# Splitting the attention's score maxima before the turn instead of after it, with two row transfers in place of six

## The reference, cut to what matters

```python
scores = jnp.einsum('bsqhd,bthd->bqhst', qh, kh) * scale
probs = jax.nn.softmax(scores, axis=-1)
a_dot = jnp.einsum('bqhst,bthd->bsqhd', probs, vh)
```

## Time and profile before

| what | value |
|---|---|
| median of 3 runs | 823.25 us (820.08 to 824.85) |
| the profiled execution, its own time | 819.99 us |
| its span in the profile | 818.1 us |
| PE busy | 734.5 us (90%) |
| DVE busy | 484.8 us (59%) |
| ACT busy | 413.3 us (51%) |
| POOL busy | 150.4 us (18%) |
| attention, first score matmul to last | 146.9 to 512.8 us |

### The profile page before, as it was taken

One profiled execution on the slowest core, in us unless ns is written; L12 is line 12 of the kernel. 1 busy time (PEld: TensorE's weight loads), 2 busy tenths in 40 slices (PEclk: granted clock), 3 DMA queues, 4 the chain that ended last, 5 costly groups with the idle time before them and its releaser, 6 DMA issues.

```text
span 818.1 us, 13465 instructions
## 1 busy us (share of the span) xinstructions
PE 734.5 (90%) x3824; PEld 345.9 (42%) x3825; DVE 484.8 (59%) x675; ACT 413.3 (51%) x803; POOL 150.4 (18%) x265
## 2 busy tenths in 40 slices
PE   4999999688888888888888888899999999998997
PEld 2455445211221222222221112466656565657887
DVE  4375688678889888888898880221212121215854
ACT  2473401477788777787787787422222222225432
POOL 1000001755532222121222121000000000003740
PEclk9999999889999999999999999999999999999999
DMA  9637100447210111110110361051111111111431
GB/s 315 215 97 289 30 0 15 137 141 236 83 57 16 30 30 30 30 29 17 29 30 30 91 207 64 27 193 47 43 51 39 51 38 51 38 39 59 120 100 51
DMA packets 51279, 65.35 MB, mean 80 GB/s; under 512 B 9497, under 2 KB 44209, under 8 KB 51249
## 3 DMA queue, kind: packets, MB, share of 16 engines
q1 hardware_dynamic: 40192, 40.85, 15.8%
q10 hardware_dynamic: 7984, 15.73, 5.8%
q0 software_dynamic: 3072, 8.39, 3.2%
HBM read 40.15 MB, written 24.38 MB: 79 GB/s over the span
## 4 chain that ended last, share of the span: by engine, by line
PE 69%; issue 9%; ACT 7%; DVE 5%; POOL 4%; SPq 3%; DMA 2%; ACTq 1%; DVEq 0%; POOLq 0%
PE ps L1291 16%; PE ps L1273 9%; PE ps L1360 8%; PE ps L1154 7%; ACT att L689 6%; PE ps L1314 6%; PE ps L1392 5%; DVE smax L938 4%; PE ps L1146 3%; PE ps L1407 3%; PE ps L1351 2%; SPq L388 2%; PE ps L1179 2%; PE ps L1114 2%; PE ps L1262 1%
## 5 line engine op out<-in xcount | busy, mean ns | idle before, releaser
L938 DVE TENSOR_REDUCE smax<-ps 128x2 f32<-128x1024 f32 x256 | 302.4, 1221 | 54.7 <-PE ps L1179 52.3
L689 ACT ACTIVATE att<-ps 128x512 f32<-128x512 f32 x512 | 267.7, 602 | 92.1 <-PE ps L1314 90.5
L1314 PE MATMUL ps<-att 51*128 51x512 bf16 x512 | 162.3, 388 | 55.2 <-ACT att L689 23.5
L1179 PE MATMUL ps<-att 48*128 48x512 bf16 x512 | 159.9, 389 | 1.4 <-DVE smax L938 1.4
L1314 PEld LDWEIGHTS ps<-att 51*128 51x128 bf16 x512 | 40.0, 94 | 244.9 <-ACT att L689 103.0
L1291 PE MATMUL ps<-big,xn 128*128 x312 | 140.9, 594 | 1.8 <-ACT oT_sb L662 1.2
L1273 PE MATMUL ps<-att,v_head 128*32 128x512 f32 x1024 | 138.8, 614 | 1.4 <-ACT o_sb L657 0.4
L1018 DVE COPY xn<-ps 128x512 f32<-128x512 f32 x39 | 27.0, 692 | 170.2 <-PE ps L1351 170.2
L1291 PEld LDWEIGHTS ps<-big,xn 128*128 128x128 f32 x312 | 58.9, 190 | 61.5 <-issue 59.7
L564 POOL DMA_INDIRECT xn<-slot_y,slot x32 | 33.7, 1054 | 237.3 <-DMA slot_y<-xn 227.9
L1360 PE MATMUL ps<-big,xn 128*128 x312 | 73.7, 380 | 0.1
(11 more groups left out here) (149 smaller groups left out, 642.8 us busy)
## 6 DMA issues: line engine op xcount, KB each, us to landing
big<-w ACTq DMA_DIRECT2D x8, 1024.0 KB, 5.8
q_stacks<-big SPq DMA_DIRECT2D x12, 512.0 KB
att<-q_stacks SPq DMA_DIRECT2D x64, 96.0 KB, 2.2
slot_x<-zeros SPq DMA_DIRECT2D x1, 4992.0 KB, 17.1
e_x<-slot_x SPq DMA_DIRECT2D x39, 128.0 KB, 2.0
slot_y<-xn SPq DMA_DIRECT2D x39, 128.0 KB, 1.7
big<-w ACTq DMA_DIRECT2D x8, 512.0 KB, 8.1
att<-k_stacks SPq DMA_DIRECT2D x64, 48.0 KB, 2.0
```

The source lines that it names most:

```text
L689: act.activation(probs[:, t % 2, g, :], ps[:, RING[turn_of(u) % 3], :], ACT.Exp, scale=SCALE)\
L938: dve.reduce_max(smax[:, s % 2, :].rearrange("p (half v) -> p half v", half=2)[:, :, v], ps[:, bank:bank + 2, :], X_AXIS).then_inc(max_don ...
L1179: return pe.matmul(ps[:, bank + half, :], q_st[s][rows, g, P * st:P * (st + 1)], k_st[s][rows, :], start=True, stop=True)
L1314: pe.matmul(ps[:, RING[turn % 3], :], k_st[s][rows, P * t:P * (t + 1)], q_st[s][rows, g, :], start=True, stop=True).then_inc(scores_ready, 1)
```

## The change

The maxima are split before they are turned. POOL's `split_max` reads `smax` (128 x 16) as soon as the eight reductions are done and writes three bf16 parts as columns of `max_parts` (128 x 48), again with four dependent instructions, now of 128 x 16 each. It stands ahead of `stage_v` in POOL's queue. PE turns all 48 columns with one bf16 matmul against a bf16 identity `eye`; it now waits for `m_ready` (POOL), not for `max_done` (DVE). ACT negates 48 x 128 into bf16 `neg_parts` and now waits for `m_loaded` of two steps before. SP waits for ACT's `negm_ready` and issues two DMAs of three rows each. POOL makes `eye` once at the start. DVE's first reduction of a step waits for `m_ready` instead of `maxT_in_psum`.

```diff
             def m_rows(i, s):
-                sp.wait_ge(m_ready, i + 1)
+                sp.wait_ge(negm_ready, i + 1)
                 for half in range(2):
-                    for c in range(3):
-                        row = HALF * half + R + c
-                        sp.dma_start(q_st[s % 4][row:row + 1, :, :].rearrange("o g s -> o (g s)"),
-                                     m_parts[8 * half:8 * half + 8, s % 2, c, :]).then_inc(m_loaded[s % 2], 16)
+                    first = HALF * half + R
+                    sp.dma_start(q_st[s % 4][first:first + 3, :, :].rearrange("c g n -> c (g n)"),
+                                 neg_parts[24 * half:24 * half + 24, s % 2, :]).then_inc(m_loaded[s % 2], 16)
...
+            pool.wait_ge(ident_ready, 1)
+            pool.tensor_copy(eye[:, :], ident[:, :]).then_inc(eye_ready, 1)
...
-            def split_m(i, s, pairs):
+            def split_max(i, s):
 
                 a = s % 2
-                pool.wait_ge(negm_ready, i + 1)
-                wait(pool, m_loaded[a], pairs * 96)
-                pool.tensor_tensor(m_parts[:, a, 0, :], negm[:, a, :], zeros[0:16, 0:P], ALU.subtract).then_inc(m_hi, 1)
+                whole, rest = [m.rearrange("p (half v) -> p half v", half=2) for m in (smax[:, a, :], max_rest[:, :])]
+                hi, mid, lo = [max_parts[:, a, :].rearrange("p (half c v) -> p half c v", half=2, c=3)[:, :, c, :]
+                               for c in range(3)]
+                nothing = zeros[:, 0:16].rearrange("p (half v) -> p half v", half=2)
+                pool.wait_ge(max_done, i * 8 + 8)
+                wait(pool, maxT_in_psum, i - 1)
+                pool.tensor_tensor(hi, whole, nothing, ALU.subtract).then_inc(m_hi, 1)
                 pool.wait_ge(m_hi, i + 1)
-                pool.tensor_tensor(negr[:, a, :], negm[:, a, :], m_parts[:, a, 0, :], ALU.subtract).then_inc(m_res, 1)
+                pool.tensor_tensor(rest, whole, hi, ALU.subtract).then_inc(m_res, 1)
                 pool.wait_ge(m_res, i + 1)
-                pool.tensor_tensor(m_parts[:, a, 1, :], negr[:, a, :], zeros[0:16, 0:P], ALU.subtract).then_inc(m_mid, 1)
+                pool.tensor_tensor(mid, rest, nothing, ALU.subtract).then_inc(m_mid, 1)
                 pool.wait_ge(m_mid, i + 1)
-                pool.tensor_tensor(m_parts[:, a, 2, :], negr[:, a, :], m_parts[:, a, 1, :], ALU.subtract)\
-                    .then_inc(m_ready, 1)
+                pool.tensor_tensor(lo, rest, mid, ALU.subtract).then_inc(m_ready, 1)
...
+            split_max(0, 0)
             stage_v(0, 0, 0, 0)
-            split_m(0, 0, 0)
...
                     if not (first and s == 0):
+                        split_max(i, s)
                         stage_v(i, b, h0 + s, s)
-                        split_m(i, s, blk * 2 + s // 2)
...
-            def negate_max(i, s):
+            def negate_max(i, s, pairs):
                 act.wait_ge(maxT_in_psum, i + 1)
-                wait(act, m_ready, i - 1)
-                act.activation(negm[:, s % 2, :], ps[0:16, RING[MAX_AT % 3], 0:P], ACT.Copy, scale=-1.0)\
+                wait(act, m_loaded[s % 2], pairs * 32)
+                act.activation(neg_parts[:, s % 2, :], ps[0:48, RING[MAX_AT % 3], 0:P], ACT.Copy, scale=-1.0)\
                    .then_inc(negm_ready, 1)
...
                 if v == 0:
-                    wait(dve, maxT_in_psum, i - 1)
+                    wait(dve, m_ready, i - 1)
...
             def transpose_max(i, s):
-                pe.wait_ge(max_done, i * 8 + 8)
+                pe.wait_ge(m_ready, i + 1)
                 bank_free(i - 1, MAX_AT)
-                pe.transpose(ps[0:16, RING[MAX_AT % 3], 0:P], smax[:, s % 2, :], ident[:, :])\
+                pe.matmul(ps[0:48, RING[MAX_AT % 3], 0:P], max_parts[:, s % 2, :], eye[:, :], start=True, stop=True)\
                   .then_inc(maxT_in_psum, 1)
...
-                pe.wait_ge(m_loaded[s % 2], blk * 192 + 96 * (s // 2 + 1))
+                pe.wait_ge(m_loaded[s % 2], blk * 64 + 32 * (s // 2 + 1))
```

More of the change, by code:

```diff
@@ L127, in build @@
         smax = sb("smax", [P, 2, 16])
-        negm = sb("negm", [16, 2, P])
-        negr = sb("negr", [16, 2, P])
-        m_parts = sb("m_parts", [16, 2, 3, P], BF16)
+        max_parts = sb("max_parts", [P, 2, 48], BF16)
+        max_rest = sb("max_rest", [P, 16])
+        neg_parts = sb("neg_parts", [48, 2, P], BF16)
+        eye = sb("eye", [P, P], BF16)
         rden = sb("rden", [P, 2, 32])
@@ L197, in build @@
         ident_ready = sem("ident_ready")
+        eye_ready = sem("eye_ready")
         consts_ready = sem("consts_ready")
@@ L676, in exps @@
                     if u == 4 and not last:
-                        negate_max(i + 1, s + 1)
+                        negate_max(i + 1, s + 1, blk * 2 + (s + 1) // 2)
                     if u == 7 and last:
@@ L697, in _ @@
             LATE = {-4: (4, 5), -3: (6,), -2: (7,), -1: ()}
-            negate_max(0, 0)
+            negate_max(0, 0, 0)
             for i in range(4):
@@ L1089, in _ @@
             pe.wait_ge(ident_ready, 1)
+            pe.wait_ge(eye_ready, 1)
             def transpose_xn(g):
```

## The result

The changed kernel took 824.59 us (median; 821.97 to 827.34). The kernel before, run beside it on the same chips, took 817.45 us (811.80 to 827.62). The ratio is 1.0083 (95% interval 1.0064 to 1.0102): slower by 0.8%, where 817.4 us and a gain had been forecast. The profiled execution took 826.23 us, its span is 824.4; against the one before, 819.99, that is 6.2 us more.

What follows compares the result with a forecast made beforehand. PE owned most of the chain of waits, with SP's issues of maxima rows 2%. Won 8.6 us, lost 2.8, net 5.8: 819.99 to 814.2 us profiled, 817.4 on the median's scale; range 809 to 825.

Steps and rivals of the forecast that it cites:

- The even stalls: PE's waits for the maxima rows at even step starts, costing about 0.54 us each; all were to go.
- S: Serial path from last reduction to turn: hand-over to POOL, four instructions, three gaps, hand-over to PE; 1.30 us.
- the wait only moves: Rival, chance 0.10: at 0.23 us per POOL instruction a pair costs 0.62, eating the 8.6 won: 823 us.
- the part on steps 1 to 5: Early steps: 2.0 us won in step 1 and 2.4 in steps 2 to 5, part stalls, part half clock ending.
- The prediction's own sign of being wrong: A pair shorter than 22.0 or longer than 23 us, step 1 starting after 160, or PE waiting for rows again.
- start of step 1: Step 1 begins at 157.6, not 161.85, as its rows land before the expert weights start: 4.2 us won.
- step 1: Step 1 falls from 12.65 us to 10.62, an odd step without the stall at its end: 2.0 won.
- steps 2 to 5: They took 46.91 us where two ordinary pairs take 44.52: 2.4 won, from stalls and half clock.
- pairs of steps, from step 6 to 27: Each pair costs 0.20 us more: odd steps 0.56 later, even ones 0.36 earlier; +2.2 us here.
- steps 28 to 30: End of the attention: the same 0.20 us lost per pair of steps, +0.2 us here.
- The early stretch gives less: Rival, chance 0.20: half clock may come from expert weights, or rows still land late behind them; about 820 us.
- Slower: Rival, chance 0.10: short POOL instructions mostly fixed cost, every turn waits for the split; 831 us at 0.30 us each.

Runs made afterwards that it cites:

- the best version: The late turn's kernel with the split for step 1 moved ahead of POOL's eight additions: 800.52 us, ratio 0.9789; on a third chip 797.16 us, ratio 0.9754.
- the kernel with filler in odd steps: Changed kernel with two unread matmuls of 384 columns before PE's wait for the split, in odd steps only: 817.10 us, ratio 1.0004.
- the fifth instruction: Changed kernel with a fifth dependent POOL instruction in the split (the second one made twice): 840.90 us, ratio 1.0278.
- six transfers: Changed kernel with six transfers of one row each again, in place of two of three rows: 824.90 us, ratio 1.0008.
- the control of the filler: Changed kernel with two unread matmuls of 384 columns before PE's wait for the split, in even steps only: 827.47 us, ratio 1.0126.
- the late turn: Changed kernel with the turn of the maxima put behind the first weighted values in PE's queue: 800.92 us, ratio 0.9717; repeated, 801.10 us, ratio 0.9793.

## Why the prediction was wrong

**What held.** The even stalls went. S was 1.24 to 1.42 us, mostly 1.32, forecast 1.30 (step 28 aside, where other waits hold the turn). The weighted values follow the turn after 0.16 us, forecast 0.155. A pair at full clock takes 22.46 to 22.54 us, forecast 22.46. Two issues take 1.47 us, forecast 1.3 to 4. POOL's instruction was mis-sized a little, 0.22 us for 0.18, which alone would have made S 1.46; the hand-over to POOL took 0.08 where 0.20 was taken, and that to PE 0.13. The nearest of the prediction's rivals in size, "the wait only moves", set the point from which a pair costs 0.62 at 0.23 us an instruction and S = 1.51; the instruction came near it and S did not. From the figures of the Trainium skill (GPSIMD Engine Reference, section 3.1) the prediction had worked out an estimate of 0.095 us. The trace does not agree with it: 0.22 us at 16 elements.

**What failed.** The step is in the part on steps 1 to 5: "I take it that it stays at 2.4 GHz when the stalls are gone, as it did in the steps that lost only 0.5 us." It was costed for those five steps and not looked at for the others. The stalls of 0.5 us were not gone but moved: an even step had lost 0.47 to 0.55 us at its start, and an odd step now loses 0.57 or 0.65 us right behind another wait of 0.89 us. Nine times out of fourteen (the odd steps 3 to 29) 3.4 us at half clock followed, 1.17 us each; with 0.50 us of the pause filled none did. The row of that wait was in the earlier trace rows. The comparison with steps "that lost only 0.5 us" took a stall by itself; here two come within 2.8 us. The prediction's own sign of being wrong came true by it: a pair of steps 6 to 27 took 23.25 us on average, above 23. The sum in the profile:

| term | forecast | measured |
|---|---|---|
| start of step 1 | -4.2 | -2.9 |
| step 1 | -2.0 | -2.4 |
| steps 2 to 5 (2.4 won, 0.4 lost to two pairs) | -2.0 | -0.9 |
| pairs of steps, from step 6 to 27 | +2.2 | +10.9 |
| steps 28 to 30 | +0.2 | +1.6 |
| sum | -5.8 | +6.3 |

Of the +10.9, 11 pairs at +0.24 (22.50 against 22.26) are 2.6, and seven stretches at 1.17 are 8.2. The half clock of step 5 takes the 1.1 that are missing in steps 2 to 5, that of step 29 makes most of the 1.6. Step 1 started at 158.94 and not at 157.6: step 0 has the wait for POOL, forecast in its size (2.42 us for 2), and a half-clock stretch behind it (from 151.7). That the wait brought this one is not shown, since one profile of the best version has such a stretch without the wait; by the two profiles of that version it costs 1.42 us. Taken off, nine stretches at 1.17 and this one at 1.42, the +6.3 become -5.6, where -5.8 was forecast: in the profiles nearly the whole error is clock.

Of the medians this explains less. The kernel before had a median of 817.45 us over 20 runs, 2.5 below its own profiled execution, where the prediction had set it 3.3 above; the early stalls that the change removes, read from that one execution, were probably of its longer ones. That the forecast's 817.4 and the 817.10 us of the kernel with filler in odd steps agree is therefore partly chance: by its ratio that kernel is equal to the one before, not faster, and its step 0, with 6.8 us of half clock, took 13.04 us where 157.6 - 146.88 = 10.7 had been forecast.

**The rivals.** "The early stretch gives less" took the half clock for an effect of the expert weights' traffic. Steps 3 and 4 refute it: granted clock 1.00 at a DMA share of 0.70, and 0.50 at 0.02 to 0.30 elsewhere. "Slower" had the right sign by the wrong mechanism, POOL instructions of 0.27 us and more, where 0.22 was measured; the fifth instruction shows that a longer split has such a price (0.30 us a step). The cause of the loss, half clock in odd steps, had no rival and no chance of its own.

**Open.** Odd steps 9, 11, 17 and 19 have the same waits as 13 and 15 and kept full clock. Which steps fall differs: with six transfers it was 9, 11, 13, 19, 25 and 27, in the control of the filler 11, 19, 21 and 23. What decides it was not settled. It was not tried to shorten the 0.89 us wait for the reduction instead, so the new pause alone was not measured. Step 0 has half clock with and without a wait for POOL, and its cause is open too.

## What to carry to other kernels

When a wait is moved, look for the waits that it comes to stand beside: two short pauses of a busy PE close together can bring half clock, and this can cost more than the moved wait does as time (here 8.2 us against 2.6 in steps 6 to 27), so sum the idle time of PE by stretch and not only by cause, before and after. Put the consumer of a new serial chain where work in its own queue covers the chain; here one moved line turned a loss of 0.8% into a gain of 2.1 to 2.8%. And before building a new way round a late producer, ask what is ahead of it in its own queue: a swap of two lines on POOL gave 1.1% by itself.

## What was not expected of the hardware

- Two pauses, of 0.89 and 0.57 or 0.65 us (0.96 and 0.48 in steps 3 and 29), within the first 2.8 us of a step were followed by 3.4 us at half clock in nine of the fourteen odd steps from 3 to 29. The 0.89 us by itself, as with the late turn, was followed by none in steps 1 to 30. In the Trainium skill (TensorE: Matmul & The Clock Gate, Part 1) the clock gate follows how busy the array has been. The trace agrees in kind: the granted clock was 0.50 behind the two pauses, and 1.00 in steps 1 to 30 where 0.50 us of the second was filled.
- Adding 0.50 us of useless matmuls to the pause of every odd step made the kernel 7.5 us faster; the same matmuls in the even steps did not (827.47 us for 824.59).
- A GpSimd instruction with two inputs took 0.22 us at 16 elements, 0.416 at 128 and 0.72 at 256: by these three nearly all of the 0.22 us is fixed cost (an estimate). A dependent one follows after 0.08 us.
- One issue of three rows took 0.73 us (1.47 / 2), against 0.67 for one row.
